# Cross-attention and quantized FFN on one core: the value weights in quarters at the start, and another order of the last tiles at the end

## The reference

```python
x = x + xattn(layernorm(x), ctx)        # x: (4, 512, 1024), ctx: (4, 64, 1024)
x = x + ffn(layernorm(x))
# xattn: hidden = concat([ctx, latents]);  q = latents @ Wq.T,  k, v = hidden @ Wk.T, hidden @ Wv.T
#        16 query heads of 96, 4 key/value heads; softmax(q k / sqrt(96)) v, then @ Wo.T
# ffn:   gate, up = qlinear(x, w_gate), qlinear(x, w_up);  qlinear(silu(gate) * up, w_down), inner width 2752
# qlinear: rows of x and rows of w are rounded to whole numbers in -128..127 with a scale max|row| / 127 each
```

## Time and profile before

| | before |
|---|---|
| device time, median of 3 runs | 1581.5 us (1580.5 to 1582.52) |
| profiled execution: device time | 1579.16 us |
| profiled execution: span | 1577.5 us |
| PE busy | 1500.4 us, 95% of the span |
| DVE, ACT, POOL busy | 1104.9, 635.1, 649.6 us (70%, 40%, 41%) |
| mean granted clock of PE | 0.991 of 2.4 GHz |

### The profile page before, as it was taken

One profiled execution on the slowest core, in us unless ns is written; L12 is line 12 of the kernel. 1 busy time (PEld: TensorE's weight loads), 2 busy tenths in 40 slices (PEclk: granted clock), 3 DMA queues, 4 the chain that ended last, 5 costly groups with the idle time before them and its releaser, 6 DMA issues.

```text
span 1577.5 us, 23750 instructions
## 1 busy us (share of the span) xinstructions
PE 1500.4 (95%) x7985; PEld 747.4 (47%) x7985; DVE 1104.9 (70%) x2012; ACT 635.1 (40%) x1164; POOL 649.6 (41%) x845
## 2 busy tenths in 40 slices
PE   5999989999998999999899999979899999999997
PEld 2544445554443555444465544434444444444443
DVE  5355664666686567768576666773899999999984
ACT  4356555555454545546455545551211111111110
POOL 4187775554667654557654556671000000000000
PEclk9999999999999999999999999999999999999998
DMA  7299999879999987899998999999934233332332
GB/s 241 79 256 220 245 241 213 183 180 241 283 275 201 221 197 160 220 296 247 225 201 199 229 253 267 234 212 263 307 96 110 65 95 99 85 96 78 85 96 58
DMA packets 487084, 297.82 MB, mean 189 GB/s; under 512 B 405789, under 2 KB 443985, under 8 KB 485841
## 3 DMA queue, kind: packets, MB, share of 16 engines
q1 hardware_dynamic: 486993, 296.68, 76.0%
HBM read 143.13 MB, written 46.69 MB: 120 GB/s over the span
## 4 chain that ended last, share of the span: by engine, by line
PE 74%; SPq 8%; DMA 7%; DVE 4%; issue 2%; POOL 2%; ACT 2%; DVEq 0%; ACTq 0%
PE ps_s L1570 17%; PE ps_g L1603 10%; PE ps_g L935 10%; PE ps_g L937 10%; PE ps_g L936 10%; PE ps_s L1031 7%; SPq L807 4%; PE ps_o L1047 3%; PE ps_o L1048 3%; DMA pT<-p_nat 3%; PE ps_o L1050 2%; SPq L787 1%; DMA xnT<-xh 1%; POOL p_nat L910 1%; PE ps_s L1032 1%
## 5 line engine op out<-in xcount | busy, mean ns | idle before, releaser
L910 POOL TENSOR_TENSOR p_nat<-p_f,p_nat 128x512 f16<-128x512 f32 x256 | 309.4, 1209 | 140.8 <-ACT p_nat L1147 140.3
L905 POOL TENSOR_SCALAR p_f<-p_f,small 128x576 f32<-128x576 f32 x256 | 201.8, 788 | 273.9 <-DVE small L1261 272.9
L1136 ACT ACTIVATE p_f<-ps_s,small 128x576 f32<-128x576 f32 x256 | 188.6, 737 | 257.4 <-DVE small L1256 252.7
L1256 DVE TENSOR_REDUCE small<-ps_s 128x1 f32<-128x576 f32 x256 | 191.4, 748 | 101.8 <-PE ps_s L1032 100.7
L1031 PE MATMUL ps_s<-k,q 96*128 96x512 f16 x768 | 224.6, 382 | 22.2 <-ACT p_f L1136 19.1
L1570 PE MATMUL ps_s<-w_gu_sb,xT 128*128 128x512 bf16 (+1 forms) x1152 | 226.5, 357 | 5.4 <-DVE g_sb L1690 4.1
L1623 ACT ACTIVATE g_sb<-g_sb,sx 128x512 f32<-128x512 f32 (+1 forms) x128 | 74.5, 582 | 381.1 <-DVE g_sb L1690 331.6
L1147 ACT ACTIVATE p_nat<-p_f 128x576 f16<-128x576 f32 x256 | 172.7, 676 | 111.2 <-POOL p_f L905 60.6
L1555 POOL TENSOR_TENSOR rstd<-var_eps,minus_half 128x1 f32<-128x1 f32 x16 | 8.8, 548 | 425.1 <-DVE var_eps L1645 425.1
L1603 PE MATMUL ps_g<-w_dn_sb,hT 128*128 128x512 bf16 x704 | 162.4, 384 | 6.1 <-DMA hT<-h_int 5.3
L1570 PEld LDWEIGHTS ps_s<-w_gu_sb,xT 128*128 128x128 bf16 x1152 | 112.3, 98 | 117.2 <-DVE g_sb L1690 8.8
(11 more groups left out here) (114 smaller groups left out, 2465.9 us busy)
## 6 DMA issues: line engine op xcount, KB each, us to landing
w_in<-w_gu SPq DMA_DIRECT2D x40, 512.0 KB, 4.8
wq<-wq_c SPq DMA_DIRECT2D x36, 512.0 KB, 4.8
wo<-wo_c SPq DMA_DIRECT2D x24, 768.0 KB, 6.2
gu_q<-w_t SPq DMA_DIRECT2D x44, 256.0 KB, 4.7
w_in<-w_dn SPq DMA_DIRECT2D x8, 1376.0 KB, 7.1
x_acc<-x SPq DMA_DIRECT2D x4, 2048.0 KB, 9.0
x<-x_acc SPq DMA_DIRECT2D x8, 1024.0 KB, 6.0
x_ln<-x SPq DMA_DIRECT2D x16, 512.0 KB, 3.6
```

Of the source, the lines that this page charges most:

```text
L905: nc.gpsimd.tensor_scalar(f, f, inv_sum[:, j % 2, t:t + 1], P_UP, ALU.mult, ALU.mult).then_inc(p_scaled, 1)
L910: nc.gpsimd.tensor_tensor(h[:, S + C:2 * S], f[:, 0:T], h[:, 0:T], ALU.subtract)
L1136: nc.scalar.activation(p_f[:, tile(b, j, t) % NF, :], scores(t), ACT.Exp, bias=neg_max[:, j % 2, t:t + 1], accum_out=sums[:, j % 2, t:t + ...
L1256: nc.vector.tensor_reduce(neg_max[:, j % 2, t:t + 1], scores(t), AX.X, ALU.max, negate=True).then_inc(mx_done, 1)
```

## The change

At the beginning the value weights are loaded, split and used in four quarters. They have semaphores of their own, so no quarter waits for a buffer, and later items of the stage list shift by two numbers. DVE makes the low halves of the two contexts in place of POOL. The splits, the token chain and the loads stand in another order on each engine: DVE normalises tile 0 ahead of the first weight split, SP issues the key weights only behind the transposes of tiles 0 and 1, and the bank evacuations of V0 to V2 come ahead of the key weights' split. At the end the loops stop earlier (PE's two iterations, DVE's one), and the rest is written out: half of down(13) runs between gates(14) and gates(15), the other half behind gates(15), then down(14) and down(15). The last two `hT` lie in the region of the first gates' weights (`w_first`), which is free once quarter 0 of gates(15) has run; the last `xT` is the buffer `xT0`, which only tile 0 used. Tile 14's residual lies in `x_ln`. down(15) works in pieces of 512, 256 and 256 columns in three banks, each with its own store. In every tile `x_quant` moves from behind the products and the maximum of quarter 2 to ahead of them.

The names at the head of the file, and PE's part of a quarter of `PAIR`:

```diff
+PARTS_V = 4
+QUARTER = KD * KV * HD // PARTS_V
...
-                    pe.wait_ge(ctx_lo, contexts(None, 1))
+                    if part == 0:
+                        pe.wait_ge(ctx_lo, contexts(None, 1))
                     freed(pe, ITEM["wv", part])
...
-            for part in range(parts(u)):
-                unit[u[0]]((None, u), part, parts(u))
+            n = PARTS_V if u == PAIR else parts(u)
+            for part in range(n):
+                unit[u[0]]((None, u), part, n)
```

SP at the beginning:

```diff
         stage(0)
+        tokens(None, 1)
         context(None, 1)
-        tokens(None, 1)
         stage(1)
         tokens(None, 2)
+        stage(2)
+        stage(3)
         tokens(None, 3)
         sp.dma_start(early_wq, wqT[0, :, 0:D]).then_inc(e_in[0], EV)
+        turn_tokens(None, 0)
+        turn_tokens(None, 1)
         sp.dma_start(early_wk, wkT).then_inc(e_in[1], EV)
-        for t in range(TT):
-            turn_tokens(None, t)
-        stage(2)
-        stage(3)
+        turn_tokens(None, 2)
+        stage(PARTS_V)
+        turn_tokens(None, 3)
+        stage(PARTS_V + 1)
```

ACT at the beginning:

```diff
         w_split(0)
+        tokens_hi(None, 0)
         context_hi(None, 1)
-        tokens_hi(None, 0)
         w_split(1)
+        w_split(2)
         tokens_hi(None, 1)
+        w_split(3)
         tokens_hi(None, 2)
         tokens_hi(None, 3)
         evac(None, PRO[0])
         early_split(0)
-        evac(None, PRO[1])
+        for u in PRO[1:4]:
+            evac(None, u)
+        w_split(PARTS_V)
```

DVE at the beginning, with the subtraction that POOL did (POOL's two calls of `context_lo(None, ...)` are gone):

```diff
+        def first_context_lo(i):
+            cols = slice(T + i * C, S + i * C)
+            dve.wait_ge(ctx_hi, contexts(None, i))
+            nc.vector.tensor_tensor(xnT_lo[:, :, cols], context_tile(None, i), xnT_hi[:, :, cols], ALU.subtract).then_inc(
+                ctx_lo, 1)
...
+        norm_tokens(None, 0)
+        first_context_lo(0)
         w_split(0)
-        norm_tokens(None, 0)
         norm_stats(None, 1)
+        first_context_lo(1)
+        norm_tokens(None, 1)
         w_split(1)
-        norm_tokens(None, 1)
         norm_stats(None, 2)
+        w_split(2)
+        norm_tokens(None, 2)
+        w_split(3)
         norm_stats(None, 3)
-        norm_tokens(None, 2)
         norm_tokens(None, 3)
```

The buffers and pieces of the end:

```diff
+    hT_last = [w_first[:, i * IC * P:(i + 1) * IC * P].rearrange("p (c n) -> p c n", c=IC) for i in range(2)]
+    LAST = TILES - 1
+    PIECES_OUT = ((0, 512), (512, 256), (768, 256))
```

SP at the end:

```diff
+            other = isinstance(t, int) and t in (0, LAST)
+            if other and t:
+                sp.wait_ge(gu_done, NUSE)
+            elif not first:
                 sp.wait_ge(gu_done, t * NUSE)
             elif t == 1:
...
+        def res_before_last():
+
+            sp.wait_ge(x_q, TILES + 1)
+            sp.dma_start(x_ln[:], x2[(LAST - 1) * P:LAST * P, :]).then_inc(res_in, EV)
+
+        def store_last():
+            for i, (a, n) in enumerate(PIECES_OUT):
+                c = slice(a, a + n)
+                sp.wait_ge(r_done, LAST * 2 + 3 + i)
+                sp.dma_start(out[LAST * P:TILES * P, c], x_res[:, c]).then_inc(out_s, EV)
+
+        def h_transpose(t, last=None):
 
             sp.wait_ge(h_q, t + 1)
-            sp.wait_ge(d_done, t * 2)
+            if last is None:
+                sp.wait_ge(d_done, t * 2)
+            else:
+                sp.wait_ge(gu_done, LAST * NUSE + QU)
             sp.nop(nofuse=True)
-            sp.dma_start_transpose(hT[:], h_int[:]).then_inc(h_turned, EV)
+            sp.dma_start_transpose((hT if last is None else hT_last[last])[:], h_int[:]).then_inc(h_turned, EV)
...
+        x_transpose(LAST)
+        h_transpose(LAST - 1, 0)
+        res_before_last()
+        h_transpose(LAST, 1)
+        store(LAST - 2)
+        res_tile(LAST, LAST - 1)
+        store(LAST - 1, x_ln)
+        store_last()
```

PE at the end:

```diff
+        def down_last():
+
+            pe.wait_ge(h_turned, TILES * EV)
+            for i, (a, n) in enumerate(PIECES_OUT):
+                if i < 2:
+                    pe.wait_ge(d_read, LAST * 2 + (i + 1))
+                for c in range(IC):
+                    rows = P if c < IC - 1 else I_LAST
+                    mm = nc.tensor.matmul(kept.ps_g[i][:, 0:n], hT_last[1][0:rows, c, :],
+                                          w_dn[0:rows, c // KC, a // 32:(a + n) // 32,
+                                               c % KC * 32:(c % KC + 1) * 32],
+                                          start=(c == 0), stop=(c == IC - 1))
+                mm.then_inc(d_done, 1)
...
-        with pe.Fori(0, TILES - 2) as t:
+        with pe.Fori(0, TILES - 4) as t:
             gates(t + 2)
             down(t + 1)
-        down(TILES - 1)
+        gates(LAST - 1)
+        down(LAST - 2, halves=(0,))
+        gates(LAST, xT0)
+        down(LAST - 2, halves=(1,))
+        down(LAST - 1, False, hT_last[0])
+        down_last()
```

DVE in every tile (inside `gates(t, nxt)`), and at the end:

```diff
+                if nxt is not None and q == 2:
+                    x_quant(nxt, turned)
                 product(t, q, 0)
...
+        def result_last():
+
+            dve.wait_ge(h_small, LAST * NH + 16)
+            dve.wait_ge(res_in, TILES * EV)
+            for i, (a, n) in enumerate(PIECES_OUT):
+                c, u = slice(a, a + n), u_sb[:].rearrange("p h c -> p (h c)")[:, a:a + n]
+                dve.wait_ge(d_done, LAST * 2 + (i + 1))
+                nc.vector.scalar_tensor_tensor(u, kept.ps_g[i][:, 0:n], sh_last[:], s_dn[:, c], ALU.mult,
+                                               ALU.mult).then_inc(d_read, 1)
+                dve.wait_ge(d_read, LAST * 2 + (i + 3))
+                nc.vector.tensor_tensor(x_res[:, c], u, x_res[:, c], ALU.add).then_inc(r_done, 1)
...
+        gates(LAST - 1, LAST, LAST * EV)
+        h_part(LAST - 1, LAST * EV - EV)
+        next_x_scale()
+        result(LAST - 2, (0,))
+        gates(LAST)
+        h_part(LAST, LAST * EV, sh_last)
+        result(LAST - 2, (1,))
         next_h_scale()
-        result(last + 1)
+        result(LAST - 1, x_res=x_ln)
+        result_last()
```

95 lines of the change are left out of this document (42 added, 53 removed).

## The result

The changed kernel takes 1571.85 us (median of 7 executions, 1566.76 to 1575.47) against 1581.76 us for the kernel before on the same chip: ratio 0.9944, 95% interval 0.9925 to 0.9964. One of the seven executions of the kernel before took 2285 us and stands outside the ratio, which for that reason is not exactly the quotient of the two medians. Two further comparisons gave 0.9939 (0.9917 to 0.9962) and 0.9922 (0.9900 to 0.9944). The first median lies nearer to the first rival's 1572.5 (the beginning gives nothing) than to the forecast, so the time alone does not tell the two apart; the traces do. The profiled execution has a span of 1570.1 us, before 1577.5, at a mean granted clock of 0.992.

What follows compares the result with a forecast made beforehand. PE's back-to-back matmuls were taken as the bound, with waits at both ends. End 9.1 plus beginning 3.7 made 12.8 us off the profiled 1579.16; with the median 2.3 higher, 1568.7 us, range 1565 to 1573.5.

Steps and rivals of the forecast that it cites:

- first rival: Beginning: gaps in quartered `PAIR` keep PE slow through V0, 3.9 us lost, beginning gives nothing; 1572.5 us, chance 0.15.
- (a): End: with separate buffers the last hidden tile's transpose lands 12.0 us behind the gates, under 14.7 of downs; 5.25 saved.
- (b): Last gates: DVE, 4.0 us late, catches up with 4.9 us free, so the cover holds; PE waits 0.1 us.
- The input tile: Last gates: moved `x_quant` lets tile 15's transpose land at 1519.9, before 1521.35; unmoved it would be 0.4 us late.
- third rival: Loop: moved `x_quant` delays PE by up to 1.43 us in 14 tiles, 20 us; 1588.7 us, chance 0.04.
- (c): Last down: at full clock and in three pieces it takes 10.1 us in place of 12.86; 2.75 saved (1.85 to 3.05).
- (d): Tail: smaller DVE operations and last store leave 3.4 us behind the last matmul, not 4.63; 1.2 saved (0.1 to 2.0).
- The beginning: Start of program: V2 and V3 no longer wait, queries start near 36.5 in place of 40.23; 3.7 us won.
- A transpose of over 6 us: Beginning: sign that the forecast is wrong, if the transposes of tiles 2 and 3 take that long; 4.4 us was expected.
- second rival: End: cover of the last transpose fails, 2.6 us of wait and 2.75 of slow clock stay; 1574.1 us, chance 0.1.
- The weighing of the subtraction on DVE: Beginning: context subtractions on DVE wait behind POOL, fourth split ends at 20.8, 3.0 us won not 3.7; against the move.
- The middle: Between the two ends: same instructions in the same order, nothing by absolute time, so it shifts as a whole.

Runs made afterwards that it cites:

- no_half: Changed kernel with tile 13's down product undivided ahead of the last gates, the separate hidden-tile buffers kept: 1572.85 us in one execution.
- xq_old: Kernel with old beginning and new end, but `x_quant` back behind the products and maximum of quarter 2: 1573.80 us, ratio 0.9956 to the kernel before.
- v0_fill: loads_late plus three quarters of V0 put ahead of the fourth quarter of `PAIR` on PE: 1569.95 us, ratio 0.9923 to the kernel before.
- ctx_pool: Changed kernel with the low halves of the two contexts computed on POOL again in place of DVE: 1572.01 us in one execution.
- loads_late: Changed kernel with transposes of tiles 2 and 3 issued ahead of the last query block and key weights loads: 1568.76 us, ratio 0.9915 to the kernel before.
- wk_early: Changed kernel with the 1536 KB key weights load issued ahead of the transposes of tiles 0 and 1: 1567.7 us in one execution.
- begin_only: Changed kernel with the old loops and end restored, keeping only the new beginning: 1579.08 us, ratio 0.9989 to the kernel before.
- before: The kernel before the change, in its first profiled execution: span 1577.5 us; median 1581.76 us beside the changed kernel.
- after_third: The changed kernel unaltered, run a third time on the chip of v0_fill: 1569.74 us, ratio 0.9922 to the kernel before.
- after: The changed kernel in its first comparison with the kernel before: median 1571.85 us, ratio 0.9944; profiled span 1570.1 us.
- before_again: The kernel before the change, unaltered, run once more for a second trace: 1582.93 us in one execution.

## Why the prediction was right, and where it was off

**(a) and (b), the wait and its cover: right.** The whole wait of 5.25 us is gone, with no wait in its place. The order of events is that of the sum: the hidden tile is ready 6.8 us behind the last gates (1547.16 + 1.59 - 1541.98), and PE has 14.77 us of downs. `no_half` shows the sum from the other side: with 4.9 us less cover the wait is 2.25. It also shows that the buffers alone do not do it. The transpose lands at 1548.84 + 5.16 = 1554.0, 2.7 us ahead of the last down, the slack of the sum. DVE was 3.5 us late at gates(15) and not 4.0. The 0.1 us for the bank is nothing.

**The input tile: the mechanism was there, the size was not.** I had the unmoved `x_quant` make PE wait 0.4 us. `xq_old` shows 0.9 us of slack, because this one transpose lands in 3.0 us; I had taken the median of all five, 4.1. It takes 3.0 us in every one of the fourteen executions, the first of the kernel before included (issued at 1517.69). The input transposes ahead of it take 3.8 to 4.3, each with a load of 512 KB issued 0.6 us before it, and the last has no such load. So the move of `x_quant` is worth nothing here, and it costs nothing in the loop, as forecast; the third rival (20 us) is out.

**(c) and (d): right.** Last down 10.19 against 10.1, saved 2.67 for 2.75. Behind it 1570.1 - 1566.94 = 3.2 us against 3.4, saved 1.5 for 1.2. The end is 9.4 against 9.1 in the profiled pair. The old end is not a fixed number, though: 81.9, 81.1 and 81.5 in three executions, since its last down takes 12.86, 12.01 and 12.41 (9.82 at the full clock), by how late the clock comes back: 5.8, 4.1 and 4.9 us behind the start of the down. Its mean is 81.5 and the gain 8.8.

**The beginning: 1.0 us was missing, in two steps.** The queries came at 37.57 in place of 36.5. The step "4.4 us for a transpose ... with the 512 KB load that now stands ahead of it 32.6, just where PE gets to V3" was mis-sized: it priced the load at 1.3 us. With that load issued 1.0 to 1.2 us ahead the transpose takes 6.5 to 7.05 us in six executions; without a load in flight it takes 4.3 to 4.5 in six, so the price is 2.0 to 2.7. One execution does not fit: `v0_fill` has no load ahead and takes 6.0, and no run says why. The delay makes V3 wait 0.5, 0.9, 1.6 and 1.8 us in four executions with this beginning (0.7 in `ctx_pool`), and not in `no_half`, where V0 itself ended late enough. A transpose of over 6 us was one of the prediction's own signs of being wrong, and it came. `loads_late` takes the wait away. The cleaner evidence that loads hold up transposes is tile 2's, with the 1536 KB of key weights in flight: 5.7 to 5.9 us in all six executions with them, 4.2 in `loads_late` and in `v0_fill`.

The other step is V0 at 21.41 for 20.8: 0.7 us are the fourth quarter of `PAIR`, whose matmuls lie 0.28 us apart on the mean and not 0.16. I had written 1.0 to 1.9 us for a quarter, but the range of V0, 20.6 to 21.1, is worked out with the 1.0 alone; with 1.9 it goes to 22.0. The fourth quarter itself began at 19.72, inside the 19.6 to 20.1 of the sum. (The range has a slip of the same kind: 1573.1 for all bounds at their worst comes out with 2.2 us for the beginning; with its own lower bound of 1.5 it is 1573.8.)

**The first rival was partly right.** It had 24 slow matmuls in V0, 3.9 us. In all three executions of the changed kernel V0 has none, in `loads_late` and `no_half` five to seven, in `wk_early` about three. So the mechanism is real and worth 0 to 1.0 us in V0, and up to 0.9 more in the last quarter of `PAIR`. The rows show three courses with the same matmuls in the same order. The pace stays at 0.32 us until 21.2 (first execution of the changed kernel, and `begin_only`). Or it goes to 0.16 near 15.3 and stays there (the second and third). Or it goes to 0.16 by the third quarter and back to 0.32 behind the idle 1 us ahead of the fourth (`loads_late`, `wk_early`, `no_half`). The second and third execution have the same idle time and keep the full pace, so the gap does not decide by itself. `v0_fill` fills the place of the gap, but while the pace was still 0.32, and so cannot say whether filled time keeps the full pace. The second rival (1574.1) did not come.

**The weighing of the subtraction on DVE went the wrong way.** The rows of the changed kernel show that DVE and POOL wait for each other, DVE first:

```profile
10.96 1.06 DVE L1239 TENSOR_TENSOR xnT<-xc,xnT 128x512 f16<-128x512 f32 x1
15.77 1.77 DVE L1217 SCALAR_TENSOR_TENSOR w_first<-w_in,w_first 128x768 f16<-128x768 f32 x1
```

```profile
11.44 1.00 POOL L894 TENSOR_TENSOR small<-small,minus_half 128x1 f32<-128x1 f32 x1
14.45 2.27 POOL L902 TENSOR_TENSOR xh<-x_acc,xh 128x512 f16<-128x512 f32 x2 [2.02 <-ACT xh L1172]
16.68 1.26 POOL L894 TENSOR_TENSOR small<-small,minus_half 128x1 f32<-128x1 f32 x1
```

POOL's second half of `xh` ends near 16.7; a split with nothing in its way takes 0.87 us to the start of the next operation (8.40 to 9.27) and this one ends at 17.54, so it began to work near 16.7. POOL's power, 0.56 alone (at 6.47), begins at 16.68 and ends behind 17.54. The rule by which I spoke against the move is that of the Trainium skill, "SBUF — State Buffer", section "SBUF: two separate sides": a DVE operation with two SBUF inputs and a GpSimd operation that reads SBUF shut each other out for a whole instruction. By that rule, the trace agrees, in both directions. But it decides nothing here: the fourth split was done by 19.72, not at 20.8. `ctx_pool`, in one execution and against POOL's order as it stood, prices the move at 40.50 - 38.0 = 2.5 us (38.0 is the mean of the five executions with the new beginning as it is), which is about all of what the beginning gains: POOL paces the token chain, a context costs it 1.15 us, and DVE's later normalisations wait 0.45, 0.45 and 1.42 us for POOL's powers.

**The middle** takes 1427.0, 1431.8, 1427.9, 1429.3 and 1429.4 us in five executions with the old beginning (mean 1429.1), and 1426.9 to 1431.8 in nine with the new one (mean 1429.6). So it scatters by 5 us under either beginning, and most of the +4.6 us of the first pair was chance. The means differ by 0.5 us; with this scatter a cost of the new beginning of up to 2 us (an estimate from the fourteen values) is not ruled out. What it is made of, worked out from the matmul records and the clock's: idle is the sum of all distances between matmuls above 0.6 us, less 0.2 each, and low the time at 1.2 GHz.

| | middle | idle | low | idle + low / 2 |
|---|---|---|---|---|
| before | 1427.0 | 53.1 | 20.5 | 63.4 |
| wk_early | 1426.9 | 50.0 | 27.3 | 63.7 |
| no_half | 1427.8 | 52.1 | 23.9 | 64.1 |
| after_third | 1429.8 | 56.5 | 20.5 | 66.8 |
| after | 1431.6 | 56.4 | 23.9 | 68.4 |
| before_again | 1431.8 | 58.6 | 20.5 | 68.9 |
| begin_only | 1431.8 | 52.6 | 34.1 | 69.7 |

These are seven of the fourteen executions; over all of them the middle less the last column stays between 1361.8 and 1364.1 us. One place in it is a wait for the probabilities' transpose behind head 12; here are PE's waits in the stretch from 230 us to head 16, first of the kernel before, then of the changed one's second execution:

```profile
PE ps_o L1047 <- DMA pT<-p_nat: 1.3, 1, 1.3
```

```profile
PE ps_o L1056 <- DMA pT<-p_nat: 3.7, 1, 3.7
```

Why that transpose is late in one execution and not in the other, no run settles.

**The sum.** By the stretches the end is worth 81.5 - 72.7 = 8.8 us. The queries start at 38.0 on the mean with the new beginning as it is (37.57, 37.81, 38.19, 38.23 and 38.41). With the old one they start at 40.23 and 40.00 in the kernel before, and at 41.25, 40.70 and 41.37 in the three kernels that have the old beginning and the new end. So the beginning is worth 40.7 - 38.0 = 2.7 against all five and 2.1 against the kernel before alone, and the two ends give 11.5 or 10.9 us, against 12.8 forecast; the three pairs of medians give 9.9, 10.4 and 12.5. The 0.5 to 1.4 us between the two groups arise before PE works: the first half of the value weights lands at 7.2 to 7.5 us in the kernel before and at 7.9 to 8.6 in the three. In all eleven executions with the new end PE's first matmul comes at 12.2 us or later, in all three with the old end at 12.05 or earlier. No run here shows why, or that it is more than chance. With the loads moved behind the transposes the medians are 1568.76 (1569.95 with V0 in the gap), beside 1569.74 of the changed kernel on the chip of the latter. V3's wait is gone in both traces, but the times do not tell these kernels from the changed one.

That the forecast of the time fell so near is in part luck: the beginning gave 1.0 to 1.6 us less than its 3.7, and the middle, which the prediction let shift as a whole, moves a single execution by up to 5 us.

## What to carry to other kernels

At the end of a program count for each late result what work the matmul engine still has, from the moment its input is finished; here 14.8 us against 12.0 made a wait vanish and 9.8 made one of 2.25, which cost 4.0 with the clock. Issue the transpose that the engine will want next ahead of plain loads on the same queue. And where two engines shut each other out, ask first which of the two paces the chain: taking two operations of 1.15 us off that one was worth more than the waits it made on the other.

## What I had not expected of the hardware

- A plain load in flight holds up the transpose that follows it: 512 KB issued 1.1 us ahead came with 2.0 to 2.7 us more, 512 KB issued 0.6 us ahead of a transpose of an input tile (`xT`) with 1 us more (3.8 to 4.3 against 3.0), and 1536 KB issued 4.5 us ahead with about 4 us more for the transpose of tile 0 (10.0 against 6.2 in the changed kernel). One transpose without a load ahead took 6.0 us all the same (`v0_fill`).
- With the same matmuls in the same order their distance falls from 0.32 to 0.16 us near 15.3 us in one execution and near 21.2 in another, and in three executions it goes back to 0.32 behind an idle time of 1 us. The changed kernel had 23 slow matmuls in its first execution and 9 in its second and third. The Trainium skill, "TensorE: Matmul & The Clock Gate", section "What's actually happening", says that the number of slow matmuls at the start varies between runs of one kernel; the traces agree.
- An idle time of 2.25 us of PE came with a stretch at the lower clock behind it: 1.8 us lost on a down of 10.2 (`no_half`). An idle time of 2 us ahead of V2 in the kernel before (32.44) did not: V2 steps by 0.16.
- A small store ends only about a microsecond sooner than one four times its size: 1.8 to 1.9 us for 128 KB, 2.0 to 2.5 for 256, 2.6 to 3.0 for 512.
